# Experts of a small transformer layer: first product by halves of the rows, three blocks of the second product in the same period, bias rows and first weights fetched early

## The reference, cut to what matters

```python
def _moe_forward(x, Wr, w1, b1, w2, b2):          # 4608 tokens, D=192, 8 experts, 2 of them for each token
    capacity = int(Bz * Sz / Ez * 1.5)             # 864 rows for each expert
    probs = jax.nn.softmax(x @ Wr, axis=-1)
    topk_p, topk_i = jax.lax.top_k(probs, 2)
    topk_p = topk_p / topk_p.sum(-1, keepdims=True)
    ...                                            # cw: the two weights of a token, zero past the capacity
    hidden = jax.nn.gelu(jnp.einsum('bsd,edh->bseh', x, w1) + b1, approximate=False)   # 768 wide
    expert_out = jnp.einsum('bseh,ehd->bsed', hidden, w2) + b2
    return jnp.einsum('bse,bsed->bsd', cw, expert_out)
```

## Time and profile before

| | |
|---|---|
| median of 3 runs | 860.81 us (859.82 to 864.62) |
| profiled execution | 862.2 us, span 860.5 us |
| busy over the span | PE 85%, DVE 74%, ACT 69%, POOL 60% |
| granted TensorE clock, mean | 0.940 |
| third block, first SP issue to end | 638.29 to 860.5 us |

### The profile page before, as it was taken

The page is one execution under the profiler, slowest core; times in us unless marked ns, Lnnn a source line. Parts: engine busy times, 40 slices in busy tenths (PEclk is TensorE's granted clock), DMA queues, the critical chain, the costliest instruction groups (busy, mean ns, idle before and its releaser), DMA issues. The chain is left out here.

```text
span 860.5 us, 25391 instructions
## 1 busy us (share of the span) xinstructions
PE 735.7 (85%) x9539; PEld 611.6 (71%) x9539; DVE 639.1 (74%) x1831; ACT 590.9 (69%) x1383; POOL 512.7 (60%) x612
## 2 busy tenths in 40 slices
PE   3689489999999999999999999975106899999994
PEld 3689257888788888888888888864103577777774
DVE  6892368899999999999999999876304666666651
ACT  1775168888888888888888888862105866766760
POOL 7666325556577687777877777775520154545555
PEclk9899699999999999999999999997557999999998
DMA  8961112111011221222212111220126466664223
GB/s 275 238 164 32 41 57 63 36 37 40 12 45 49 52 58 26 52 52 50 55 34 50 49 40 43 43 59 15 36 83 186 131 132 145 144 145 91 29 28 40
DMA packets 97034, 63.60 MB, mean 74 GB/s; under 512 B 48046, under 2 KB 91547, under 8 KB 96656
## 3 DMA queue, kind: packets, MB, share of 16 engines
q1 hardware_dynamic: 85648, 51.24, 23.0%
q0 software_dynamic: 11264, 10.74, 7.7%
HBM read 39.60 MB, written 24.15 MB: 74 GB/s over the span
## 5 line engine op out<-in xcount | busy, mean ns | idle before, releaser
L1892 POOL DMA_INDIRECT out<-y,tok x56 | 91.6, 1635 | 133.1 <-DVE y L1852 125.2
L1506 POOL TENSOR_TENSOR pl<-p,ph 128x384 f16<-128x384 f32 x144 | 131.6, 916 | 40.5 <-ACT ph L1361 38.0
L1343 ACT ACTIVATE p<-sps,nm 128x144 f32<-128x144 f32 (+1 forms) x432 | 128.7, 390 | 9.9 <-DVE nm L879 9.0
L658 PE MATMUL pj<-xt,wqkvh 128*128 128x256 f16 x648 | 108.4, 277 | 3.9 <-ACT xt L1397 1.5
L1866 DVE TENSOR_TENSOR h<-g,h 128x432 f16<-128x432 f32 x96 | 58.3, 607 | 68.8 <-ACT h L1810 68.7
L1555 POOL DMA_INDIRECT xg_d<-rows,sli x64 | 65.3, 1021 | 43.6 <-DVE sli L1206 34.4
L889 DVE COPY pt<-ptp 128x896 f16<-128x896 f16 (+1 forms) x144 | 86.2, 609 | 4.0 <-PE ptp L719 2.2
L917 DVE SCALAR_TENSOR_TENSOR qk<-pj,qk 128x512 f16<-128x512 f32 x108 | 73.8, 683 | 17.3 <-ACT qk L1326 16.4
L879 DVE TENSOR_REDUCE nm<-sps 128x3 f32<-128x432 f32 (+1 forms) x144 | 82.1, 591 | 4.5 <-PE sps L703 4.2
L1361 ACT ACTIVATE ph<-p 128x384 f16<-128x384 f32 x144 | 74.3, 537 | 15.0 <-PE ptp L719 13.6
L658 PE MATMUL pj<-xt,wqkvl 128*128 128x256 f16 x432 | 83.7, 276 | 0.0
(11 more groups left out here) (251 smaller groups left out, 2394.0 us busy)
## 6 DMA issues: line engine op xcount, KB each, us to landing
stage<-in_L_ffn_w SPq DMA_DIRECT2D x16, 384.0 KB
xg_d<-zrow SPq DMA_DIRECT2D x8, 588.0 KB, 6.1
xg<-xg_d SPq DMA_DIRECT2D x8, 588.0 KB
stage<-in_L_ffn_w SPq DMA_DIRECT2D x8, 576.0 KB, 6.0
out<-h SPq DMA_DIRECT2D x36, 96.0 KB
vi<-vimg_d SPq DMA_DIRECT2D x192, 16.2 KB
hin<-in_txt SPq DMA_DIRECT2D x16, 192.0 KB, 2.9
hres<-in_txt SPq DMA_DIRECT2D x16, 192.0 KB, 3.0
```

The source lines that it names most:

```text
L658: mm = pe.matmul(bank[:, t * 256:(t + 1) * 256], (wqkvh, wqkvl)[w][:, b, c:c + P], xt[:, q, e, :], start=i == 0, stop=i == 4)
L1343: i = a.activation(p32[:, u % 2, r, lo:SEQ], sps[u % 2][:, r * SEQ + lo:(r + 1) * SEQ], ACT.Exp, bias=nm[:, u % 2, r:r + 1])
L1506: g.tensor_tensor(pl[:, u % 2, :, :], p32[:, u % 2, :, IT:SEQ], ph[:, u % 2, :, :], ALU.subtract).then_inc(S["pll"], 1)
L1892: g.indirect_dma_start(out, bass.IndirectOffsetOnAxis(ap=tok[0:n, 1 - par, u, :], axis=0), y2[0:n, 1 - par, u, :], None, compute_op=ALU.ad ...
```

## The change

- F1 is walked by halves: first all six `m` for rows 0 to 431, then all six for rows 432 to 863 (`hf, m = divmod(q, 6)`; before `m, hf = divmod(q, 2)`).
- Blocks 0, 1, 2 (rows 0 to 383) of the second product are done in the expert's own period, at `q` 9, 10, 11; blocks 3 to 6 in the next, at `q` 0, 2, 3, 5. Block 0 waits for six low parts, block 3 for all twelve.
- The load of `b2s` moves to attention step 1, into the enlarged tile `zbuf` that held the zeros for the prefill. `w1` of expert 0 is loaded in step 15, and `w2` of expert 0 and `w1` of expert 1 in step 16 (before: `w1` of expert 0 in step 17, the others in the third block).
- The splits of these (`w2h`/`w2l` of expert 0, `b2r`, `w1h`/`w1l` of expert 1) move from periods -1 and 0 to the end of the attention block, on ACT and DVE, behind the split of `w1` of expert 0. Their tiles overlay the attention's `qk`, which stands first in its pool now.

```diff
-        zrow = sb("zrow", [P, NB, ROW], I32)
+        zbuf = sb("zbuf", [P, NE * D], I32)
+        zrow = zbuf[:, 0:NB * ROW].rearrange("p (b n) -> p b n", b=NB)
+        b2s = zbuf[:, :].bitcast(F32).rearrange("p (e n) -> p e n", e=NE)
...
+        def load_w2(sp, n, place):
+            wait(sp, "w2d", 16 * n)
+            sp.dma_start(stage[:, place, 3 * FF:].rearrange("p (c n) -> p c n", n=D),
+                         w2[bass.ds(n, 1)].rearrange("o (c p) n -> p (o c) n", p=P)).then_inc(S["w2d"], 16)
...
-            if s == NPAIR - 1:
+            if s == 1:
+                sp.dma_start(zbuf[:, :].bitcast(F32), b2.rearrange("(o e) n -> o (e n)", o=1).broadcast_to((P, NE * D))).then_inc(S["b2d"], 16)
+            if s == NPAIR - 3:
                 load_w1(sp, 0, 0)
+            if s == NPAIR - 2:
+                load_w2(sp, 0, 0)
+                load_w1(sp, 1, 1)
...
-        F2AT = {0: 0, 2: 1, 4: 2, 6: 3, 8: 4, 9: 5, 11: 6}
+        F2AT = {0: (1, 3), 2: (1, 4), 3: (1, 5), 5: (1, 6), 9: (0, 0), 10: (0, 1), 11: (0, 2)}
...
                 for b in range(3):
                     w1_hi(a, 0, 0, b)
+                for z in range(2):
+                    w2_hi(a, 0, 0, z)
+                wait(a, "b2d", 16)
+                a.activation(b2r[:, :, :], b2s, ACT.Copy).then_inc(S["b2h"], 1)
+                for b in range(3):
+                    w1_hi(a, 1, 1, b)
...
                 for b in range(2):
                     w1_lo(v, 0, 0, b)
+                for z in range(2):
+                    w2_lo(v, 0, 0, z)
+                wait(v, "b2h", 1)
+                v.tensor_tensor(b2r[64:P, :, :], b2s[64:P, :, :], b2r[64:P, :, :], ALU.subtract).then_inc(S["b2l"], 1)
+                for b in range(2):
+                    w1_lo(v, 1, 1, b)
...
-                if one:
+                if one and n > 1:
                     wait(sp, "w1hd", 3 * (n - 1))
                     wait(sp, "w1ld", 2 * (n - 1))
                     load_w1(sp, n, place)
...
-                    m, hf = divmod(q, 2)
+                    hf, m = divmod(q, 6)
...
-                if two and q in F2AT:
-                    u, tt, pr = F2AT[q], t - 1, 1 - par
+                if q in F2AT and (one, two)[F2AT[q][0]]:
+                    lag, u = F2AT[q]
+                    tt, pr = t - lag, (par + lag) % 2
+                    if u == 3:
+                        wait(pe, "hld", NQ * (tt + 1))
                     if u == 0:
-                        wait(pe, "hld", NQ * (tt + 1))
+                        wait(pe, "hld", NQ * tt + 6)
...
-                if one and q in (1, 2):
+                if one and t and q in (1, 2):
+                    w2_hi(a, t, par, q - 1)
...
-                if two and q - 1 in F2AT:
-                    second(F2AT[q - 1])
+                if two and q == 0:
+                    second(1, 2)
+                if q - 1 in F2AT and (one, two)[F2AT[q - 1][0]]:
+                    second(*F2AT[q - 1])
```

More of the change, by code:

```diff
@@ L503, in build @@
         att = ExitStack()
+        qk = sb("qk", [P, 2, 2, 6, 2, 2, SEQ], F16, att)
         hin = sb("hin", [P, 2, 2, D], F32, att)
@@ L511, in build @@
         xt = sb("xt", [P, 2, 3, 2 * P], F16, att)
-        qk = sb("qk", [P, 2, 2, 6, 2, 2, SEQ], F16, att)
         kimg = sb("kimg", [P, 2, 6, NI * IT], F16, att)
@@ L595, in w1_lo, with w2_hi, w2_lo @@
                                    w1h[:, place, b, :], ALU.mult, ALU.subtract).then_inc(S["w1ld"], 1)
+        def load_w2(sp, n, place):
+            wait(sp, "w2d", 16 * n)
+            sp.dma_start(stage[:, place, 3 * FF:].rearrange("p (c n) -> p c n", n=D),
+                         w2[bass.ds(n, 1)].rearrange("o (c p) n -> p (o c) n", p=P)).then_inc(S["w2d"], 16)
+        def w2_hi(a, n, place, z):
+            c = 3 * z
+            wait(a, "w2d", 16 * (n + 1))
+            wait(a, "f2d", NB * (n - 1))
+            a.activation(w2h[:, place, c:c + 3, :], stage[:, place, 3 * FF + c * D:3 * FF + (c + 3) * D]
+                         .rearrange("p (c n) -> p c n", n=D), ACT.Copy, scale=WS).then_inc(S["w2hd"], 1)
+        def w2_lo(v, n, place, z):
+            c = 3 * z
+            wait(v, "w2hd", 2 * n + z + 1)
+            v.scalar_tensor_tensor(w2l[:, place, c:c + 3, :], stage[:, place, 3 * FF + c * D:3 * FF + (c + 3) * D]
+                                   .rearrange("p (c n) -> p c n", n=D), WS, w2h[:, place, c:c + 3, :], ALU.mult,
+                                   ALU.subtract).then_inc(S["w2ld"], 1)
         def isb(p):
@@ L1664, in step_sp @@
             store_h(2)
-            if s == NPAIR - 1:
+            if s == 1:
+                sp.dma_start(zbuf[:, :].bitcast(F32), b2.rearrange("(o e) n -> o (e n)", o=1).broadcast_to((P, NE * D))).then_inc(S["b2d"], 16)
+            if s == NPAIR - 3:
                 load_w1(sp, 0, 0)
+            if s == NPAIR - 2:
+                load_w2(sp, 0, 0)
+                load_w1(sp, 1, 1)
+        att.close()
+        w2h = sb("w2h", [P, 2, 6, D], F16)
+        w2l = sb("w2l", [P, 2, 6, D], F16)
+        b2r = sb("b2r", [P, NE, D], F16)
+        xg = sb("xg", [P, 2, NB, ROW], I32)
+        xgt = sb("xgt", [P, 2, 3, CAP], F16)
+        wsel = sb("wsel", [P, 2, 3, NB], F32)
+        tok = sb("tok", [P, 2, NB, 1], I32)
+        g32 = sb("g32", [P, 2, HALF], F32)
+        h16 = sb("h16", [P, 2, 2, 6, CAP], F16)
+        y2 = sb("y2", [P, 2, NB, D], F32)
+        f1b = [pj[0], pj[1], ops]
+        f2b = [po[:, :], ptp[0][:, :].bitcast(F32)]
+        xtb = [b[:, :].bitcast(F16) for b in sps]
+        NX = (NB + 1) // 2
+        F2AT = {0: (1, 3), 2: (1, 4), 3: (1, 5), 5: (1, 6), 9: (0, 0), 10: (0, 1), 11: (0, 2)}
+        PREP0 = 7
         def run(f):
@@ L1706, in _ @@
                 run(lambda s, par: step_pe(pe, s, par))
[L1707 to L1724, removed]
-        F2AT = {0: 0, 2: 1, 4: 2, 6: 3, 8: 4, 9: 5, 11: 6}
-        PREP0 = 7
         def m_sp(sp, t, par, prep, one, two):
@@ L1731, in m_sp @@
                 n, place = t + 1, 1 - par
-                e = bass.ds(n, 1)
-                if one:
+                if one and n > 1:
                     wait(sp, "w1hd", 3 * (n - 1))
@@ L1741, in m_sp @@
                 sp.dma_start(xg[0:CAP - FB * P, place, FB, :], xg_d[bass.ds(n * CAP + FB * P, CAP - FB * P), :]).then_inc(S["xld"], 16)
[L1742 to L1749, removed]
+                if one:
+                    wait(sp, "w2hd", 2 * (n - 1))
+                    wait(sp, "w2ld", 2 * (n - 1))
+                    load_w2(sp, n, place)
         def m_pe(pe, t, par, prep, one, two):
@@ L1794, in m_act @@
         def m_act(a, t, par, prep, one, two):
-            if prep and not one:
-                wait(a, "b2d", 16)
-                a.activation(b2r[:, :, :], b2s[:, :, :], ACT.Copy).then_inc(S["b2h"], 1)
             for q in range(NQ):
                 if one:
-                    m, hf = divmod(q, 2)
+                    hf, m = divmod(q, 6)
                     wait(a, "f1d", NQ * t + q + 1)
@@ L1810, in m_act @@
                     a.activation(h16[:, par, 0, m, hf * HALF:(hf + 1) * HALF], g32[:, q % 2, :], ACT.Copy).then_inc(S["hhd"], 1)
-                if one and q in (1, 2):
[L1812 to L1817, removed]
+                if one and t and q in (1, 2):
+                    w2_hi(a, t, par, q - 1)
+                if prep and one and t and q in (4, 5, 6):
                     w1_hi(a, t + 1, 1 - par, q - 4)
@@ L1843, in choose, with second @@
                     v.tensor_tensor(wsel[r, par, 2, b], wsel[r, par, 0, b], wsel[r, par, 1, b], ALU.add).then_inc(S["sel"], 1)
-            def second(u):
-                tt, n = t - 1, BLK[u]
+            def second(lag, u):
+                tt, pr, n = t - lag, (par + lag) % 2, BLK[u]
                 wait(v, "f2d", NB * tt + u + 1)
@@ L1851, in second @@
                     wait(v, "add", 16 * NB * (tt - 1))
-                v.tensor_scalar(y2[0:n, 1 - par, u, :], f2b[u % 2][0:n, 0:D], wsel[0:n, 1 - par, 2, u:u + 1], 1.0 / WS, ALU.mult,
+                v.tensor_scalar(y2[0:n, pr, u, :], f2b[u % 2][0:n, 0:D], wsel[0:n, pr, 2, u:u + 1], 1.0 / WS, ALU.mult,
                                 ALU.mult).then_inc(S["y2d"], 1)
             if prep and not one:
-                wait(v, "b2h", 1)
-                v.tensor_tensor(b2r[64:P, :, :], b2s[64:P, :, :], b2r[64:P, :, :], ALU.subtract).then_inc(S["b2l"], 1)
                 for q in range(NX):
@@ L1866, in m_dve @@
                     v.tensor_tensor(h16[:, par, 1, m, c], g32[:, q % 2, :], h16[:, par, 0, m, c], ALU.subtract).then_inc(S["hld"], 1)
[L1867 to L1873, removed]
+                if one and t and q in (2, 3):
+                    w2_lo(v, t, par, q - 2)
+                if prep and one and t and q in (5, 6):
                     w1_lo(v, t + 1, 1 - par, q - 5)
@@ L1876, in m_dve @@
                     choose()
-                if two and q - 1 in F2AT:
-                    second(F2AT[q - 1])
+                if two and q == 0:
```

(5 more changed lines are left out.)

## The result

The changed kernel takes 848.88 us in the median of 4 runs (847.28 to 850.08), the kernel before 861.02 (859.82 to 864.62): 12.1 us less, ratio 0.985 with a 95% interval of 0.983 to 0.987. A second set of 5 runs gave 848.16 against 861.83, ratio 0.985 (0.982 to 0.988). The forecast was 847.5, range 842.5 to 852.0. The profiled execution after is one of 847.28 us, span 845.5.

A forecast was written before the change was run, and what follows sets the result against it. PE bounds the middle, ACT period 0, waiting for data the start, POOL's adds the tail. +1.5 - 6.0 - 1.5 + 0 - 7.4 = -13.4 on the profiled 862.2 gives 848.8; median forecast 847.5, range 842.5 to 852.

The forecast's parts named there:

- Start (B): Start of the third block: without bias rows in DVE's queue the first F1 comes sooner, -6.0 us.
- Period 0 (C): First F1 to that of period 1: ACT loses casts, three F2 blocks come in; 19.2 instead of 20.71, -1.5 us.
- Tail (E): After the last F1: POOL's last add starts at T + 11.8 instead of T + 19.24, -7.4 us.
- The sign that the prediction named: Tail: four or five POOL adds in a row after the last F1 instead of seven.
- End of the attention (A): End of the attention block: POOL's last indirect DMAs collide with DVE's moved splits, +1.5 us, bounds 0 and +5.0.
- The walk: End of the attention: stepping POOL's last DMAs through DVE's instructions; delays of 0.27 + 0.97 + 0.37, some +1.5 us.
- rival (1): End of the attention: DVE locks POOL out, the upper bound of 5.0 us; 851, chance 0.13.
- Middle periods (D): Period 1 to the last F1: block 0's stall of 0.1 to 0.3 us against the seam's 0.32, taken as 0.
- (2): Middle periods: the uneven blocks stall, each 0.6 us a period on top is 3.6; 851, chance 0.08.
- (5): Middle periods: block 0's stall at `q` 9 eats everything; no gain from 2.2 us a period, 865 at 3; chance 0.03.
- (3): Whole kernel: more is gained, no collision, seams gone, `xg` sooner, -1.5 - 2 - 1; 843, chance 0.12.
- (4): Start: the first F1 does not move, held by something else that also ends near 653; 853.5, chance 0.04.

The follow-up runs named there:

- The parts alone: Two runs against the kernel before: only the early loads and splits, 853.18 us (ratio 0.990); only the new order of products, 857.86 us (ratio 0.995).
- the one-input run: The changed kernel with DVE's splits behind w1l of expert 0 replaced by scaled copies with one input; one run, 845.54 us.

## Why the prediction was right

- **Start (B).** As worked out, 6.0 us: DVE's copies begin 0.03 us behind the sixth transpose, and the moved loads cost nothing in the attention that the trace shows. The rows of expert 0 land 5.15 us behind SP's second issue, as before, without `w2` behind them: nothing to gain there.
- **Period 0 (C).** 19.13 us against 19.2 worked out. That it agrees to 0.1 us is in part luck: in the chain PE works without a pause from the first F1 on, F1 9 ends 12.0 us behind the first F1 instead of 11.7, and the seam of 0.3 us (what of a period is not PE's work) did not come. The parts alone show the two halves of the term: some 3.2 us less for the casts, some 1.6 more for the blocks.
- **Tail (E).** Before, the last expert's seven adds ran in a row from T + 8.1; now the first starts at T + 0.2 and the other six run in a row from T + 2.7 (worked out: T and T + 2.5). The last starts at T + 11.97 against T + 11.8. The sign that the prediction named, four or five adds in a row, did not fit its own sum, which has six. POOL's pace of 1.85 us an add, not PE's 1.57 us a block, still ends the kernel.
- **End of the attention (A).** The mechanism was right, the size too small: 2.0 instead of 1.5. The walk met the third DMA with 1.1 us of the bias half ahead and the fourth with 0.5 of w1l; it was 1.30 and 0.69. This is a slip of the sum: by the prediction's own rows the third begins at 625.86 + 0.97 + 0.27 + 0.30 = 627.40, and the bias half lasts to 628.82, 1.4 us on; redone so, the walk gives 2.1. What each lost is the rest of the DVE instruction less 0.12 us, five times out of five in the changed kernel and the one-input run: rests of 0.75, 0.39, 1.30, 0.69 and 0.47 us cost 0.63, 0.26, 1.18, 0.58 and 0.35. The upper bound, POOL locked out until DVE is through, did not come about: DVE's instructions stand end to end from 620.69 to 627.48, and POOL got in between them. The Trainium skill's page SBUF — State Buffer, section "SBUF: two separate sides", gives the lock to whoever starts first for one whole instruction; the traces agree with that as far as POOL waits, and not with the strict reading of the prediction, by which a series of DVE instructions would have kept it. That DVE is held in turn they do not show: beside POOL's DMAs its w2l, bias half and w1l took 1.42, 1.75 and 1.82 us, and 1.43, 1.75 and 1.83 behind POOL's last one. That section also names two SBUF inputs or a two-port mode as what takes the lock; here one 64-partition copy with one input held POOL too, and whether it ran in such a mode no run shows. Against rival (1) the prediction had only one collision to look at; the 22 adds of the kernel before were there too.
- **Middle periods (D).** Here the step failed that set the stall of 0.1 to 0.3 us against the seam's 0.32 and took 0. PE's side was met (7.71 us from the start of F1 4, 7.7 worked out); the way over ACT and DVE takes 8.06 us until block 0 begins, not 7.8. So the stall is 0.35 us a period, and of the seam only 0.19 went: 23.06 of work + 0.13 + 0.35 = 23.54. The place was named rightly, since moving `y` ahead of w1l took exactly the 0.35 away. It is a term of 0.9 us that was taken as 0, inside its bounds.
- Of the rivals none came about: the drain's start moved by 2.0 and not 5.0 (1), the middle lost 0.16 us a period and not 0.6 (2) or 2.2 (5), the collisions and most of the seams stayed (3), and the first F1 moved by the whole 6.0 (4).
- The forecast of 847.5 lies 1.4 below the median because A (by 0.5, the slip) and D (by 0.9) together were sized 1.4 too small.

## What to carry to other kernels

A stage that only prepares has a cost of its own at every hand-over: look at the chain of waits of the start and of the tail apart from the middle, and let an earlier period do what the tail would do with data that are already there. Work that is moved under another engine's queue is not free because its own engine is idle there: look whom it can hold up, and where the trace shows that it does, put it behind that engine's last issue. In a balanced middle, order the instructions of a side engine by who waits for them: a 0.9 us split ahead of a 0.4 us result that the matmul engine needs cost 0.35 us in each period.

## What the runs showed of the hardware

- POOL's drain at the end of the attention block took 5942 ns in all nine profiles that have that end, before and after the change, with POOL's same last DMA ahead of it. It is not one price for all blocks: at the end of the first block POOL's drain took 0.04 us. Without it the next load stood 2.25 us behind POOL's last DMA instead of 8.6 us, and 5.8 us of the time went.
- An indirect DMA of POOL that begins under a DVE instruction with both inputs in SBUF takes longer by the rest of that instruction less 0.12 us, one instruction and not a series: 1.60, 1.23, 2.15 and 1.55 us instead of 0.97, the same to 0.01 us in four profiles, and up to 1.92 instead of 1.55 us for the adds of the kernel before. Under a copy out of PSUM with 0.59 us left it took 0.99 us.
- With the new order POOL's first add of an expert waits in some periods 5.7 to 7.4 us for the landing of the adds before, where it was 4.2 us once. It cost nothing here: the period with the wait of 7.4 us lasts from 736.00 to 759.53, 23.53 us as the others, and by the tail POOL has caught up and waits for `y` again (3.4 us).
